# Second norm's columns and statistics taken into the scan's last stretch, one barrier fewer, scatter paced one batch later

## The chip, the cores and the metric

The program runs on one core of one Trainium2 chip. A core has five engines that run their own instruction streams and wait for each other only through semaphores: TensorE (PE, with its weight loads as PEld), VectorE (DVE), ScalarE (ACT), GpSimd (POOL) and SyncE (SP, which here only issues DMAs). The metric is the device time of one execution in microseconds (us). The kernel before takes 1730.65 us, the median of three runs (1730.52 to 1741.02).

## The reference

Four layers work on 4096 tokens (16 sequences of 256) of 128 numbers. Each layer normalises x and adds the outputs of a mixer and of a mixture of experts to it:

```
xn = _layernorm(x, axis=-1)
x = x + _L0_attn_ref(xn, ...) + _L0_ffn_ref(xn, ...)      # selective scan; 16 experts, 12 of them MLPs
xn = _layernorm(x, axis=-1)                               # the "second norm" of the title
x = x + _L1_attn_ref(xn, ...) + _L1_ffn_ref(xn, ...)      # causal attention; 9 experts, top 2
...
```

The mixer of layer 0 is a scan over each sequence. For each of 256 channels it keeps 16 states:

```
def step(h, t):
    dA_t, dBu_t, C_t = t
    h = dA_t * h + dBu_t
    return (h, jnp.einsum('bdn,bn->bd', h, C_t))
```

The router of layer 1 takes `sigmoid(xn @ gate.T + bias)` and the two largest of nine scores. What matters here: the mean and the variance of each token's 128 numbers, and the nine products of each normalised token with the router's columns.

## The kernel before

x stays in SBUF as `x_tok` (`g.x`), 32 tiles of 128 tokens by 128 numbers. A program is a row of blocks. Inside a block each engine runs its own stream; at a block's end all engines meet in a barrier. A `section` holds the semaphores of a block. When it ends it clears them, and unless it was told `last=False` it sets one more barrier behind that.

**Layer 0** (`mamba`) is one block in two parts. In its first part, the front, PE makes convolution and gate of 16 batches of 256 tokens (lines 662 and 666), ACT applies the activations of a batch (lines 812 and 814, counted in `act_done`), SP stores the gates, DVE makes the step sizes `delta`, and POOL scatters the tokens' rows to the experts' places in DRAM: 64 indirect DMAs, 56 of them in the front (line 591, issued by line 1048) and 8 between the first steps of the scan. The n-th scatter waits until ACT has done `3 + n // 5` batches, at most 16:

```
pool.wait_ge(fs.act_done, min(BATCH, 3 + n // 5))
scatter_choice(nc, pool, scattered, disp, g, r, n)
```

In its second part, the scan, there are 128 steps: 8 blocks of 512 tokens times 16 states. In a step ACT makes the decays (830, 832), POOL the inputs (613, into the space of `xn_t`), DVE the scan itself and the product with C (976, 984), and PE adds the product up in two PSUM banks (683). After 16 steps DVE multiplies by the gate (`gated`, 992), PE projects the block and adds x (`project`, 695 to 699), and ACT copies the sum back into `x_tok` (`take_out`, 846). Between the steps PE and ACT run the 12 experts. For the first seven of eight groups of four tiles the rows that the experts gave are added to x in steps 105 and later (`join`, 711 and 713; ACT's `take_joined`, 882, counted in `x_taken`). The eighth group is added by the last `project`, behind the last step.

**The second norm** (`normalise`, titled `norm1`) is the next block. PE turns the raw tiles of x on their side (270), ACT copies each four into `xn_t` (326), and PE multiplies them by the router's nine columns (255), which PE and ACT have centred before (276, 319) so that no mean has to be subtracted from x. DVE takes statistics of 32 tiles (212, 215), ACT the square root (303), DVE corrects it (220 to 224) and writes the 32 normalised tiles (233). Then DVE waits for all products (`logits_done`) and runs the router's choice, a chain of some forty short steps from line 1127 on. Behind it stand the barrier and layer 1's attention block, whose first matmuls are at line 1988. SP meanwhile loads the next weights, clears the experts' places and loads 4.9 MB of expert weights (`grouped_w`).

The order on each engine is the order in which its function is written; nothing is scheduled by a planner. PSUM has eight banks: the decays of even steps lie in banks 0 and 1, those of odd steps in 2 and 3, the sums in 4 and 5, the projection in 6.

Of the kernel before, what the change touches and what calls it, by code (L numbers as in the profile page):

```python
# [9 lines left out]
ALU = mybir.AluOpType  # L10
# [114 lines left out]
def normalise(nc, g, title, src, dst, dst_t, scale_col=None, bias_col=None, pool_job=None,  # L125
              router=None, n_exp=0, disp=None, arriving=(), router_scale=None, prefetch=None, second=None, raw=False,
              table=None, beside=None, have_stats=False):
# [5 lines left out]
    with section(nc, title, "cols_in", "stats_done", "aggr_done", "var_ready", "std_ready", "rstd_step", "xn_ready",  # L133
                 "turned", "t_ready", "job_done", "router_in", "router_scaled", "zeroed", "logits_done", "row_in", "r2_step",
                 "r2_sqrt", "xr_ready", "centre_set", "centred", "w_ready", *ROUTE, *MIX) as s:
        W = s.sb("router", [P, max(n_exp, 1)])
        wc = s.sb("router_scale", [P, 1])
        centre = s.sb("centre", [P, P]) if raw else None
# [15 lines left out]
        groups = 2 * NT // G if beside else NT // G  # L154
# [4 lines left out]
        with nc.Block() as block:  # L159

            @block.sync
            def _(sp):
# [5 lines left out]
                if router is not None:  # L168
                    sp.dma_start(W[:], router).then_inc(s.router_in, 16)
# [35 lines left out]
            def _(dve):  # L205
                if raw:
                    nc.vector.tensor_scalar(centre[:], g.ident[:], -1.0 / D, None, ALU.add).then_inc(s.centre_set, 1)
                if not have_stats:
                    for i in range(NT):
                        if arriving and i % (NT // len(arriving)) == 0:  # L210
                            dve.wait_ge(arriving[i * len(arriving) // NT], 16)
                        nc.vector.bn_stats(stats[:, i, :], src[:, i, :]).then_inc(s.stats_done, 1)
                    for i in range(NT):
                        dve.wait_ge(s.stats_done, i + 1)
                        nc.vector.bn_aggr(mv[:, i, :], stats[:, i, :]).then_inc(s.aggr_done, 1)
                    dve.wait_ge(s.aggr_done, NT)
# [33 lines left out]
            def _(pe):  # L250

                def logits(b):
                    pe.wait_ge(s.t_ready, b + 1)
# [10 lines left out]
                for i in range(NT):  # L264
                    b = i // G
                    if i % G == 0 and b >= LB:
                        pe.wait_ge(s.t_ready, b - LB + 1)
# [3 lines left out]
                    if i % G == G - 1:  # L271
# [7 lines left out]
                        if router is not None and b >= 2:  # L279
                            logits(b - 2)  # L280
                if router is not None:
                    logits(NT // G - 2)
                    logits(NT // G - 1)
                    pe.wait_ge(s.logits_done, NT // G)
                if job:
                    job.products(pe)
                    for i in range(NT):
                        if i % G == 0:
                            pe.wait_ge(s.t_ready, NT // G + max(0, i // G - LB + 2))
# [9 lines left out]
            def _(act):  # L299
# [16 lines left out]
                for b in range(NT // G):  # L316
# [3 lines left out]
                    act.wait_ge(s.turned, b + 1)  # L320
# [6 lines left out]
                    if raw and b == RAW_ROOTS:  # L327
                        roots()
                if job:
                    job.scalar(act)  # L330
                    for b in range(NT // G):
                        act.wait_ge(s.turned, NT // G + b + 1)
# [32 lines left out]
def mamba(nc, g, t, u, gate_d, delta, bc_d, r, disp, ybuf, scattered, f):  # L365
# [29 lines left out]
    JOINED = NB - 1  # L395
    with section(nc, "front", *ROUTE, "xz_ready", "gate_ready", "gate_out0", "gate_out1", "act_done", "biased", "added",
# [21 lines left out]
        with section(nc, "scan", *names, "skip_made", "zeroed", "du_ready", "bu_made",  # L418
                     "da_ready", "scan_done", "hc_ready", "sum_done", "yg_ready", "o_ready", "o_taken",
                     "gate_in", "b_in0", "b_in1", "b_in2", "b_in3", "c_in0", "c_in1", "c_in2", "c_in3", "ew_in0", "ew_in1", "ex_in0", "ex_in1", "ex_in2", "ex_in3", "turned", "xt_ready", "h_ready", "h_kept",  # L420
                     "act_done", "y_ready", "y_out", "stored0", "stored1", "weighted", "joined", "x_taken") as s:
            a_neg, d_col, w_out = f.a_neg, f.d_col, f.w_out
            d_diag = s.sb("d_diag", [P, DC, P])
# [50 lines left out]
            with nc.Block() as block:  # L474

                @block.sync
                def _(sp):
# [72 lines left out]
                    for q in range(NQ):  # L550
# [16 lines left out]
                        if q == Q_LOAD:  # L567
                            for p in range(2):
# [10 lines left out]
                def _(pool):  # L579
# [5 lines left out]
                    for n in range(2 * SCATTERED_IN_FRONT):  # L585
# [4 lines left out]
                        pool.wait_ge(fs.act_done, min(BATCH, 3 + n // 5))  # L590
# [35 lines left out]
                def _(pe):  # L626
# [144 lines left out]
                    for c in range(DC):  # L771
                        sum_states(NQ - 1, c)
                    for k in range(PIECES):
                        project(NB - 1, k)

                @block.scalar
                def _(act):
# [110 lines left out]
                    for q in range(NQ):  # L888
# [15 lines left out]
                        if j is not None:  # L904
                            take_joined(j)
                    take_out(NB - 1)

                @block.vector
                def _(dve):
# [27 lines left out]

                    job.vector(dve)
# [68 lines left out]
                    for q in range(NQ):  # L1007
# [423 lines left out]
def layer1(nc, g, t, m_out):  # L1431


    with ExitStack() as c:
# [18 lines left out]
        def prologue(loads, fill):  # L1453
            with section(nc, "mixes", "mix_in0", "mix_in1") as mixes:
# [6 lines left out]
                def pool_job(pool, rows_done):  # L1461
# [4 lines left out]
                          pool_job=pool_job, raw=True, table=ACT.Sigmoid,  # L1466
# [1468 lines left out]
def program(nc, t, out):  # L2935
    with ExitStack() as ctx:
# [16 lines left out]
        g.blank = sb("blank_rows", [P, BLANKS, ROW])  # L2953
        g.mv = sb("norm_mv", [P, NT, 2])
# [114 lines left out]
```

## Time and profile before

| | us |
|---|---|
| median of the three runs | 1730.65 |
| the profiled execution | 1731.69 |
| its span in the trace | 1729.9 |
| layer 0's front | 40.1 to 165.5 |
| layer 0's scan, 128 steps | 165.5 to 651.2 |
| from the last step to the second norm's block | 651.2 to 662.1 |
| the second norm until the router's choice begins | 662.1 to 683.4 |
| the router's choice, until layer 1's block | 683.4 to 704.1 |

The profiled execution spends 1.8 us outside the span. Times in the rows are counted from the start of the span; a row of a timeline merges instructions of one form that follow each other on an engine. "banks" is PSUM. What stands behind "idle before" names what ended the engine's wait.

### The profile page before, as it was taken

The page shows a single profiled execution, that of the slowest core. Times are in us where ns is not written, and L with a number is a line of the kernel's source. Part 1 is how long each engine was busy: PE and PEld are TensorE (multiplying, and loading weights), DVE is VectorE, ACT ScalarE, POOL GpSimd, SP SyncE. Part 2 cuts the span into 40 slices and gives each one's busy share as a digit, 9 for nine tenths or more (in the row PEclk, how much of TensorE's full clock was granted, in tenths as well). Part 3 has the DMA queues.
Part 4 walks back from the last instruction along what each step waited for, and adds up shares of the span by engine and source line. Part 5 has one row for each costly group of instructions (what it writes and reads, how often), then busy time and mean ns, then how long its engine had stood idle before and what let it go on. Part 6 is the DMA issues. An engine that isn't in the chain of part 4 may idle for free. (4 is left out here: it accounts for less than half of the span.)

```text
span 1729.9 us, 31949 instructions
## 1 busy us (share of the span) xinstructions
PE 1483.8 (86%) x11604; PEld 949.2 (55%) x11604; DVE 1228.4 (71%) x2007; ACT 957.3 (55%) x1608; POOL 766.5 (44%) x691
## 2 busy tenths in 40 slices
PE   5978698888887788678999999977999999878997
PEld 5745254444443337245799976632444444556885
DVE  7566999999999896666544468758823998565335
ACT  1147487786774672334665556644644777443441
POOL 1357787887887652476244443122400000055341
PEclk9989899999999897889999999986999999779999
DMA  4524776887877875675422246207621341311323
GB/s 148 159 56 124 183 184 176 185 195 187 177 178 157 202 154 194 178 183 91 76 63 63 56 91 96 35 24 187 101 60 37 58 70 27 140 38 49 88 77 103
DMA packets 193562, 200.93 MB, mean 116 GB/s; under 512 B 22474, under 2 KB 142569, under 8 KB 193152
## 3 DMA queue, kind: packets, MB, share of 16 engines
q1 hardware_dynamic: 181816, 177.33, 44.3%
q0 software_dynamic: 11520, 21.52, 4.6%
q8 instruction: 95, 1.56, 0.4%
q14 instruction: 59, 0.48, 0.1%
q10 hardware_dynamic: 72, 0.03, 0.0%
HBM read 144.45 MB, written 57.48 MB: 117 GB/s over the span
## 5 line engine op out<-in xcount | busy, mean ns | idle before, releaser
L613 POOL TENSOR_TENSOR xn_t<-scan_b_rows,scan_du 128x1024 f32<-128x1024 f32 x128 | 301.0, 2359 | 103.5 <-DMA scan_b_rows<-states 65.9
L683 PE MATMUL banks<-ring,ident 128*128 128x512 f32 x512 | 263.2, 628 | 69.3 <-DVE ring L984 68.5
L976 DVE TENSOR_TENSOR_SCAN banks<-banks,xn_t 128x1024 f32<-128x1024 f32 x128 | 293.0, 2289 | 17.8 <-ACT banks L832 16.2
L2455 ACT ACTIVATE att_pr<-banks 128x768 f32<-128x768 f32 (+1 forms) x256 | 234.1, 916 | 128.5 <-PE banks L2342 77.0
L683 PEld LDWEIGHTS banks<-ring,ident 128*128 128x128 f32 x512 | 90.0, 195 | 200.2 <-DVE ring L984 132.6
L832 ACT ACTIVATE banks<-delta,scan_exp_centre,a_neg 128x510 f32<-128x510 f32 x256 | 189.2, 770 | 0.3
L2503 DVE TENSOR_REDUCE att_mb<-banks 128x4 f32<-128x1024 f32 x128 | 154.0, 1221 | 17.1 <-PE banks L2309 11.9
L2358 PE MATMUL banks<-att_pr,att_vx 128*32 128x256 f32 (+1 forms) x2048 | 153.6, 371 | 8.3 <-ACT att_ot L2460 4.7
L2499 DVE TENSOR_REDUCE att_mb<-banks 128x6 f32<-128x768 f32 x128 | 121.4, 954 | 54.2 <-PE banks L2316 39.4
L984 DVE TENSOR_TENSOR ring<-banks,scan_c_rows 128x1024 f32<-128x1024 f32 x128 | 156.4, 1222 | 3.8
L1603 POOL IOTA xn_tok<- 128x32 int32 x1 | 0.2, 187 | 287.2 <-POOLq L80 287.2
L2309 PE MATMUL banks<-att_ks,att_qs 48*128 48x256 bf16 (+1 forms) x1024 | 108.7, 271 | 17.9 <-DMA att_ks<-k_parts 6.6
L1419 POOL DMA_INDIRECT ybuf<-att_yo,att_xin x72 | 69.9, 970 | 104.5 <-DVE att_yo L1403 94.9
L2334 PE MATMUL banks<-att_qs,att_ks 50*128 50x256 bf16 (+1 forms) x1024 | 107.1, 266 | 6.0 <-DMA att_qs<-att_mt 2.6
L1329 PE MATMUL banks<-att_xt,att_wc 128*128 128x128 f32 x864 | 109.8, 277 | 1.3 <-DVE att_xt L1384 1.3
L1329 PEld LDWEIGHTS banks<-att_xt,att_wc 128*128 128x128 f32 x864 | 103.5, 194 | 1.9 <-DVE att_xt L1384 1.7
L1048 POOL DMA_INDIRECT disp<-xn_tok,places x64 | 69.5, 1085 | 53.4 <-ACT u L814 34.3
L830 ACT COPY banks<-zeros 128x4 f32<-128x4 f32 x128 | 20.8, 162 | 114.3 <-DVE ring L984 114.3
L2276 POOL DMA_INDIRECT disp<-xn_tok,places x64 | 62.9, 983 | 42.3 <-issue 14.6
L2334 PEld LDWEIGHTS banks<-att_qs,att_ks 50*128 50x128 bf16 x1024 | 39.6, 94 | 60.1 <-issue 39.7
L1620 POOL DMA_INDIRECT ybuf<-gau_eyo,gau_exin x40 | 39.6, 991 | 72.6 <-DVE gau_eyo L1914 65.0
L1384 DVE COPY att_xt<-banks 128x128 f32<-128x128 f32 x72 | 20.9, 291 | 71.3 <-issue 45.7
(398 smaller groups left out, 3129.5 us busy)
## 6 DMA issues: line engine op xcount, KB each, us to landing
scan_b_rows<-states SPq DMA_DIRECT2D x128, 256.0 KB
scan_c_rows<-states SPq DMA_DIRECT2D x128, 256.0 KB
scan_ew<-f_packed SPq DMA_DIRECT2D x12, 578.0 KB
q_parts<-att_p_parts SPq DMA_DIRECT2D x16, 384.0 KB, 4.6
k_parts<-att_p_parts SPq DMA_DIRECT2D x16, 384.0 KB, 5.2
att_qs<-q_parts SPq DMA_DIRECT2D x64, 96.0 KB
att_ks<-k_parts SPq DMA_DIRECT2D x64, 96.0 KB
disp<-blank_rows SPq DMA_DIRECT2D x1, 4680.0 KB, 15.2
```

The costliest lines, as they stand in the source:

```text
L613: nc.gpsimd.tensor_tensor(bu[:, q % AHEAD], b_rows[:, q % HELD, None, :].to_broadcast([P, DC, TT]), du[:, b % 2], ALU.mult).then_inc(s.bu_ ...
L683: nc.tensor.matmul(g.ps[:, Y0 + c, :], g.ident[:], hc[:, q % RING, c], start=False, stop=(q % DS == DS - 1)).then_inc(s.sum_done, 1)
L832: ins = nc.scalar.activation(inner(decays(q)[:, c]), inner(delta[:, c, span(b)]), ACT.Exp, scale=a_neg[:, c, n:n + 1], bias=exp_centre[:])
L976: v.tensor_tensor_scan(states, states, rows(bu[:, q % AHEAD]), 0.0, ALU.mult, ALU.add).then_inc(s.scan_done, 1)
L984: v.tensor_tensor(hc[:, q % RING], decays(q), c_rows[:, q % HELD, None, :].to_broadcast([P, DC, TT]), ALU.mult).then_inc(s.hc_ready, 1)
L1329: ins = nc.tensor.matmul(g.ps[:, 4 * p + 1 + m, c * P:(c + 1) * P], wc[:, p, m, c * P:(c + 1) * P], xt[:, p, :], start=True, stop=True)
L2309: ins = nc.tensor.matmul(g.ps[:, 2 * m_slot(i) + half, lo:hi], qs[rows_of, p, j, q * P:(q + 1) * P], ks[rows_of, p, j, 0:hi - lo], start=T ...
L2334: ins = nc.tensor.matmul(g.ps[:, 2 * s_slot(i) + half, k * T:k * T + T - q0], ks[rows_of, p, j, k * P:(k + 1) * P], qs[rows_of, p, j, q0:T ...
L2358: ins = nc.tensor.matmul(g.ps[r * 32:(r + 1) * 32, O_BANK, q0:T], vx[:, b % 2, k, 4 * jg + r, :], pr[:, i % RING, half, k * T:k * T + T - q0],
L2455: nc.scalar.activation(pr[:, i % RING], g.ps[:, at:at + 2, 0:W], ACT.Exp, scale=scale).then_inc(s.p_ready, 1)
L2499: v.tensor_reduce(mb[:, b % 2, j, :].rearrange("p (g n) -> p g n", g=2), g.ps[:, at:at + 2, 0:W].rearrange("p g (n k) -> p g n k", k=P), A ...
L2503: v.tensor_reduce(mb[:, b % 2, j, :], g.ps[:, at:at + 2, :].rearrange("p g (n k) -> p (g n) k", k=T), AX_X, ALU.max).then_inc(s.m_taken, 1)
```

## The change

1. **The scan's last stretch.** A buffer `centre` and the router's columns (`next_router`, loaded by SP in step 102) are there before the scan ends. Behind the last `sum_states` PE centres the columns (line 782 of the changed kernel) and turns 28 tiles of x, that is the seven groups that have been joined by then (790): three groups ahead of the last `project`, four behind it. ACT copies them into `xn_t` (935), three groups ahead of its last `take_out` and four behind. DVE takes the statistics of those 28 tiles (1058, 1068), ten ahead of the last `gated`, the others behind it.
2. **The second norm** only turns, copies and measures the last four tiles. The products of the first 28 wait for nothing any more.
3. **One barrier.** The section of the scan ends with `last=False`.
4. **The scatter's pace.** The n-th scatter waits for `4 + n // 5` batches in place of `3 + n // 5`. No instruction moves by this; only the value that POOL waits for does.

On PE, before, from the end of the last `project` over the block's end (the two branches) into the second norm:

```order
L695 MATMUL banks<-w_out_m,front_dtx 128x128 x2
L696 MATMUL banks<-x_tok,ident 128x128
L699 MATMUL banks<-xn_tok,ident 128x128 x2
L474 UNCONDITIONAL_BRANCH
L249 UNCONDITIONAL_BRANCH [waits barrier_Pool_Activation_PE_DVE_SP_release]
L270 MATMUL banks<-ident,x_tok 128x128 x8
L276 MATMUL banks<-norm_router,norm_centre 128x9 [waits norm1_centre_set,norm1_router_in]
L270 MATMUL banks<-ident,x_tok 128x128 [waits norm1_w_ready]
L270 MATMUL banks<-ident,x_tok 128x128 x3
L255 MATMUL banks<-norm_router,xn_t 128x9 [waits norm1_t_ready]
L255 MATMUL banks<-norm_router,xn_t 128x9 x3
```

On PE, of the change, from the last `sum_states` (690) to the first of the last `project` (702):

```order
L690 MATMUL banks<-ring,ident 128x512 [waits scan_hc_ready]
L690 MATMUL banks<-ring,ident 128x512
L782 MATMUL banks<-next_router,scan_centre 128x9 [waits scan_next_in,scan_centre_set]
L790 MATMUL banks<-ident,x_tok 128x128 [waits scan_x_taken]
L790 MATMUL banks<-ident,x_tok 128x128 x3
L790 MATMUL banks<-ident,x_tok 128x128 [waits scan_x_taken]
L790 MATMUL banks<-ident,x_tok 128x128 x3
L790 MATMUL banks<-ident,x_tok 128x128 [waits scan_x_taken]
L790 MATMUL banks<-ident,x_tok 128x128 x3
L702 MATMUL banks<-w_out_m,front_dtx 128x128 [waits scan_weighted,scan_o_taken,scan_yg_ready]
```

On PE, of the change, from the last group turned over the block's end into the second norm:

```order
L790 MATMUL banks<-ident,x_tok 128x128 [waits scan_xt_kept,scan_x_taken]
L790 MATMUL banks<-ident,x_tok 128x128 x3
L480 UNCONDITIONAL_BRANCH
L251 UNCONDITIONAL_BRANCH [waits barrier_Pool_Activation_PE_DVE_SP_release]
L273 MATMUL banks<-ident,x_tok 128x128 x4
L258 MATMUL banks<-next_router,xn_t 128x9 x28
L258 MATMUL banks<-next_router,xn_t 128x9 [waits norm1_t_ready]
L258 MATMUL banks<-next_router,xn_t 128x9 x3
```

So 28 transposes have gone ahead of the barrier, 12 of them ahead of the last projection, and behind the barrier the products stand in one run.

On DVE, of the change, from the last step's product (1022) over the block's end into the second norm:

```order
L1022 TENSOR_TENSOR ring<-banks,scan_c_rows 128x1024 [waits scan_sum_done,scan_c_in3,scan_scan_done]
L1058 BN_STATS norm_stats<-x_tok 128x6 [waits scan_x_taken]
L1058 BN_STATS norm_stats<-x_tok 128x6 x9
L1030 TENSOR_TENSOR front_dtx<-banks,front_gate 128x1024 [waits scan_o_ready,scan_gate_in,scan_sum_done]
L1058 BN_STATS norm_stats<-x_tok 128x6 x18
L1068 BN_AGGR norm_mv<-norm_stats 128x2 [waits scan_stats_done] x28
L480 UNCONDITIONAL_BRANCH
L206 UNCONDITIONAL_BRANCH [waits barrier_Pool_Activation_PE_DVE_SP_release]
L214 BN_STATS norm_stats<-x_tok 128x6 x4
```

Before, the gate's product stood right behind the last step's, and all 32 BN_STATS behind the barrier.

The diff, cut to its core:

```diff
@@ normalise
+        have = ahead.groups if ahead else 0
+        left = NT // G - have
+        W = ahead.router if ahead else s.sb("router", [P, max(n_exp, 1)])
...
-                    for i in range(NT):
+                    for i in range(have * G, NT):
...
                 def logits(b):
-                    pe.wait_ge(s.t_ready, b + 1)
+                    if b >= have:
+                        pe.wait_ge(s.t_ready, b - have + 1)
...
                 if router is not None:
-                    logits(NT // G - 2)
-                    logits(NT // G - 1)
+                    for b in range(0 if have else NT // G - 2, NT // G):
+                        logits(b)
...
-                    if raw and b == RAW_ROOTS:
+                    if raw and b == max(have, RAW_ROOTS):
                         roots()
@@ mamba
+    TURN_BANKS, CENTRE_BANK = 3, 3
+    FIRST_STATS = 10
...
                         if q == Q_LOAD:
+                            sp.dma_start(g.ahead.router[:], t["f1_gate"]).then_inc(s.next_in, 16)
...
-                        pool.wait_ge(fs.act_done, min(BATCH, 3 + n // 5))
+                        pool.wait_ge(fs.act_done, min(BATCH, 4 + n // 5))
...
                     for c in range(DC):
                         sum_states(NQ - 1, c)
+                    pe.wait_ge(s.centre_set, 1)
+                    pe.wait_ge(s.next_in, 16)
+                    nc.tensor.matmul(g.ps[:, CENTRE_BANK, 0:E1], centre[:], g.ahead.router[:], start=True,
+                                     stop=True).then_inc(s.centred, 1)
+
+                    def turn(j):
+                        pe.wait_ge(s.x_taken, j + 1)
+                        if j >= TURN_BANKS:
+                            pe.wait_ge(s.xt_kept, j - TURN_BANKS + 1)
+                        for i in range(GRP):
+                            ins = nc.tensor.transpose(g.ps[:, j % TURN_BANKS, i * P:(i + 1) * P], g.x[:, j * GRP + i, :], g.ident[:])
+                        ins.then_inc(s.x_turned, 1)
+
+                    for j in range(TURN_BANKS):
+                        turn(j)
                     for k in range(PIECES):
                         project(NB - 1, k)
+                    for j in range(TURN_BANKS, JOINED):
+                        turn(j)
...
+                    def keep(j):
+                        if j == 0:
+                            act.wait_ge(s.scan_done, NQ)
+                        act.wait_ge(s.x_turned, j + 1)
+                        nc.scalar.copy(g.xn_t[:, j * GRP * P:(j + 1) * GRP * P], g.ps[:, j % TURN_BANKS, :]).then_inc(s.xt_kept, 1)
+
+                    act.wait_ge(s.centred, 1)
+                    nc.scalar.copy(g.ahead.router[:], g.ps[:, CENTRE_BANK, 0:E1]).then_inc(s.router_made, 1)
+                    for j in range(TURN_BANKS):
+                        keep(j)
                     take_out(NB - 1)
+                    for j in range(TURN_BANKS, JOINED):
+                        keep(j)
...
+                    nc.vector.tensor_scalar(centre[:], g.ident[:], -1.0 / D, None, ALU.add).then_inc(s.centre_set, 1)
                     job.vector(dve)
...
+                    dve.wait_ge(s.x_taken, JOINED)
+                    for i in range(FIRST_STATS):
+                        statistics(i)
                     gated(NB - 1)
+                    for i in range(FIRST_STATS, JOINED * GRP):
+                        statistics(i)
+                    for i in range(JOINED * GRP):
+                        dve.wait_ge(s.stats_done, i + 1)
+                        v.bn_aggr(g.mv[:, i, :], g.stats[:, i, :]).then_inc(s.aggr_done, 1)
@@ layer1, program
+        g.ahead.groups = NT // 4 - 1
+        g.ahead.router = sb("next_router", [P, E1])
```

## Rows read from the trace of the kernel before

**Rows 1.** Windows: stretch, length; PE, PEld, DVE, ACT, POOL busy (count); PEclk, DMA share, GB/s

```profile
165.50:651.20 485.70, 399.98 (x1278) 192.36 (x1278) 458.02 (x277) 339.02 (x597) 364.55 (x193) 0.97 0.77 179
651.20:662.10 10.90, 6.72 (x44) 5.24 (x45) 1.23 (x1) 0.61 (x2) 0.01 (x1) 1.00 0.00 0
662.10:683.40 21.30, 20.19 (x99) 19.38 (x99) 18.12 (x103) 7.24 (x12) 3.00 (x5) 0.56 0.67 223
695.00:701.00 6.00, 0.00 (x0) 0.00 (x0) 5.48 (x17) 0.00 (x0) 0.06 (x1) 0.53 0.61 258
```

**Rows 2.** Timeline of DVE: start, length, line, operation, count, idle before and its end

```profile
653.23 1.23 DVE L992 TENSOR_TENSOR front_dtx<-banks,front_gate 128x1024 f32<-128x1024 f32 x1 [2.08 <-PE banks L683]
662.26 6.28 DVE L212 BATCH_NORM_STATS2 norm_stats<-x_tok 128x6 f32<-128x128 f32 x32
668.45 2.20 DVE L215 BATCH_NORM_AGGREGATE norm_mv<-norm_stats 128x2 f32<-128x6 f32 x32
672.45 8.29 DVE L233 TENSOR_SCALAR xn_tok<-x_tok,norm_mv,norm_rstd 128x128 f32<-128x128 f32 x32
683.41 0.30 DVE L1127 MEMSET norm_cont<- 128x288 f32 x1 [2.67 <-PE banks L255]
```

**Rows 3.** Timeline of PE in the same stretch

```profile
651.21 1.98 PE L683 MATMUL banks<-ring,ident 128*128 128x512 f32 x4 [1.48 <-DVE ring L984]
654.51 0.71 PE L695 MATMUL banks<-w_out_m,front_dtx 128*128 128x128 f32 x4 [1.32 <-DVE front_dtx L992]
662.11 1.07 PE L270 MATMUL banks<-ident,x_tok 128*128 128x128 f32 x8 [2.87 <-PEq L80]
678.15 5.13 PE L255 MATMUL banks<-norm_router,xn_t 128*128 128x9 f32 x24
```

**Rows 4.** Timeline of ACT in the same stretch

```profile
645.42 0.59 ACT L882 COPY x_tok<-banks 128x512 f32<-128x512 f32 x1 [1.84 <-PE banks L713]
659.28 0.58 ACT L846 COPY x_tok<-banks 128x512 f32<-128x512 f32 x1 [11.80 <-PE banks L699]
662.08 1.28 ACT L311 ACT_TABLE_LOAD   x1 [2.21 <-PEq L80]
670.90 0.23 ACT L303 ACTIVATE norm_std<-norm_rstd 128x32 f32<-128x32 f32 x1 [4.60 <-DVE norm_rstd L218]
```

**Rows 5.** Waits of SP's queue from 655 to 664: us in total, times, longest

```profile
SPq L80 <- PEq L80: 1.7, 3, 0.7
```

**Rows 6.** Window of PE alone: length, busy us and count, PEclk, DMA share, GB/s

```profile
664.60:683.30 18.70, 18.64 (x88) 0.50 0.74 249
```

**Rows 7.** Timeline of POOL where the front meets the scan

```profile
153.06 0.97 POOL L1048 DMA_INDIRECT disp<-xn_tok,places  x1 [0.97 <-issue]
154.04 2.38 POOL L613 TENSOR_TENSOR xn_t<-scan_b_rows,scan_du 128x1024 f32<-128x1024 f32 x1
156.59 1.81 POOL L1048 DMA_INDIRECT disp<-xn_tok,places  x1 [0.17 <-issue]
```

**Rows 8.** Timelines of ACT and of DVE there: two batches' activations, the first step

```profile
151.45 0.83 ACT L814 ACTIVATE u<-banks,b_conv 128x256 f32<-128x256 f32 x2
160.24 0.83 ACT L814 ACTIVATE u<-banks,b_conv 128x256 f32<-128x256 f32 x2
165.53 2.30 DVE L976 TENSOR_TENSOR_SCAN banks<-banks,xn_t 128x1024 f32<-128x1024 f32 x1 [2.44 <-ACT banks L832]
```

**Rows 9.** Waits from 60 to 130: who for whom, us in total, times, longest

```profile
DVE delta L921 <- remote: 16.4, 1, 16.4
ACT front_gate L812 <- remote: 15.5, 2, 11.5
PE banks L645 <- DVE front_dtx L915: 12.2, 1, 12.2
```
**Rows 10.** Windows of POOL's scatters (L1048): length, busy us, count, PEclk, DMA share, GB/s

```profile
64.40:96.60 32.20, 24.79 (x25) 0.87 0.21 66
117.20:152.10 34.90, 26.08 (x23) 1.00 0.37 97
```

More of the change, by code:

```diff
@@ L126, in normalise @@
               router=None, n_exp=0, disp=None, arriving=(), router_scale=None, prefetch=None, second=None, raw=False,
-              table=None, beside=None, have_stats=False):
+              table=None, beside=None, have_stats=False, ahead=None):
     G = 4
@@ L135, in normalise @@
                  "r2_sqrt", "xr_ready", "centre_set", "centred", "w_ready", *ROUTE, *MIX) as s:
-        W = s.sb("router", [P, max(n_exp, 1)])
+        have = ahead.groups if ahead else 0
+        left = NT // G - have
+        W = ahead.router if ahead else s.sb("router", [P, max(n_exp, 1)])
         wc = s.sb("router_scale", [P, 1])
-        centre = s.sb("centre", [P, P]) if raw else None
+        centre = s.sb("centre", [P, P]) if raw and not have else None
         stats = g.stats
@@ L153, in normalise @@
         job = beside(s, s.sb) if beside else None
-        groups = 2 * NT // G if beside else NT // G
+        groups = NT // G + left if beside else left
         def row_bank(b):
@@ L167, in _ @@
                         n_cols += 16
-                if router is not None:
+                if router is not None and not have:
                     sp.dma_start(W[:], router).then_inc(s.router_in, 16)
@@ L205, in _ @@
             def _(dve):
-                if raw:
+                if raw and not have:
                     nc.vector.tensor_scalar(centre[:], g.ident[:], -1.0 / D, None, ALU.add).then_inc(s.centre_set, 1)
                 if not have_stats:
-                    for i in range(NT):
+                    for i in range(have * G, NT):
                         if arriving and i % (NT // len(arriving)) == 0:
@@ L263, in _ @@
                 turned_rows = src if raw else dst
-                for i in range(NT):
+                for i in range(have * G, NT):
                     b = i // G
-                    if i % G == 0 and b >= LB:
+                    if i % G == 0 and b >= LB and not have:
                         pe.wait_ge(s.t_ready, b - LB + 1)
@@ L278, in _ @@
                             pe.wait_ge(s.w_ready, 1)
-                        if router is not None and b >= 2:
+                        if router is not None and b >= have + 2:
                             logits(b - 2)
                 if router is not None:
-                    logits(NT // G - 2)
-                    logits(NT // G - 1)
+                    for b in range(0 if have else NT // G - 2, NT // G):
+                        logits(b)
                     pe.wait_ge(s.logits_done, NT // G)
@@ L315, in _ @@
                     act.wait_ge(s.cols_in, n_cols)
-                for b in range(NT // G):
+                for b in range(have, NT // G):
                     if raw and b == 2:
```

20 lines of the change are left out of this document (12 added, 8 removed).

## Prediction

> **What bounds the kernel now.** I read the windows by stage first. In the scan VectorE (DVE) is busy 458.0 of 485.7 us, TensorE (PE) 400.0 and GpSimd (POOL) 364.6 [rows 1]; the scan is bound by DVE, and the change adds nothing to its steps. Behind the last step that ends: from 651.2 to 662.1 DVE works 1.2 us of 10.9, and in the second norm until the routing begins PE is busy 20.2 of 21.3 us [rows 1]. These two stretches, 32 us in all, are what the change works on, and a timeline shows what ends last in each.
>
> The first stretch is a chain: the last step's product releases the sums, which run from 651.21 to 653.19, DVE's `gated` 653.23 to 654.46, the projection from 654.51, ScalarE's (ACT) last copy 659.28 to 659.86 [rows 2 to 4]. Until 662.1 nothing computes: that is three barriers, seen in SP's waits as three of 1.7 us together, longest 0.7 [rows 5]. In the second stretch DVE is done with its normalised rows at 680.74 (672.45 + 8.29) and then waits 2.67 us for the router's products, whose last 24 passes end at 683.28; the routing starts at 683.41, 21.3 us behind the block's start [rows 2, 3]. So PE bounds this stretch, with DVE 2.7 us behind it.
>
> **The change, part by part.** The sum is made against the profiled execution, 1731.69 us, which lies 1.04 above the median.
>
> *End of the scan.* PE gets one matmul of nine columns and 12 turns between the last sums and the last projection. Eight turns at the full clock took 1.07 us [rows 3], so 12 take 1.6. They start at 653.2 where PE idled for 1.32 us [rows 3], and end at about 654.8 in place of 654.51: +0.3 on the chain. What they wait for is there: the seventh group was added to x by 646.0 [rows 4]. The projection then ends 0.3 later, at 659.55, and ACT's own last copy at 660.13. Behind it stand four more copies of 512 columns. A copy of that size takes 0.58 [rows 4], PE's sixteen turns (2.1 us) run ahead of them, so ACT ends at 660.13 + 4 x 0.58 = 662.45 in place of 659.86: **+2.6**. Were the projection's turns late behind each copy (three banks, four groups) it would be a few tenths more; if PE's turns fit wholly in the gap, 2.3.
>
> DVE's additions cost nothing here. Statistics took 6.28 / 32 = 0.196 each [rows 2]; ten are 1.96 us and lie in the 2.08 us in which DVE waited for the last sums [rows 2]. Eighteen more (3.5) and 28 aggregations of 2.20 / 32 = 0.069 (1.9) run from 654.5 to about 660, under the projection and 2.4 us ahead of ACT's end. Were that cover gone they would cost 5.4. The three early copies on ACT (1.74) and the router's copy lie in its 11.80 us of idleness ahead of 659.28 [rows 4]. The centre is one DVE instruction at the front's start, in a pause. The router's columns are one more small DMA on SP's queue in step 102, far from any use.
>
> *One barrier fewer.* Three waits of 1.7 us are 0.57 each, the longest 0.7: **-0.6** (bounds -0.5 and -0.7) [rows 5]. The next block starts at 662.45 + 1.6 = 664.1, two microseconds later than before.
>
> *The second norm.* DVE's path: four statistics and aggregations 1.1 us. The root follows later: ACT loads a table (1.28) and now copies the last group (0.58) ahead of the roots, so the root starts at about 2.1 and takes 0.23; DVE's rows began 1.32 behind the root's end (671.13 to 672.45) and last 8.29 [rows 2, 4]. That gives 2.1 + 0.23 + 1.32 + 8.29 = 11.9 behind the block's start: the earliest the routing can begin.
>
> PE's path: four turns (0.55), then 64 passes of nine columns (two per tile) without a wait but one. Their price hangs on the clock. Before, the granted clock was 0.50 from 664.6 on (1.2 GHz of the two levels, 1.2 and 2.4), although PE was busy 18.64 of 18.70 us [rows 6]; the mean of 0.56 over the whole 21.3 us [rows 1] leaves 1.00 for the first 2.5. At 0.50 a pass took 5.13 / 24 = 0.214 us [rows 3]; at full clock I estimate half, 0.107. All at full clock: 0.55 + 6.85 + 0.13 (from the last product to the routing's first instruction, as before) = 7.5, and DVE's 11.9 is what counts. All at half: 1.0 + 13.7 + 0.13 = 14.8. With the clock falling 2.5 us after the block's start as before: 18 passes by then, 46 x 0.214 = 9.85 after, 2.5 + 9.85 + 0.13 = 12.5. I take this, since the same kind of work stands behind the same pause of PE: 12.5 in place of 21.3, **-8.8** (bounds -9.4 and -6.5).
>
> The Trainium skill ("TensorE: Matmul & The Clock Gate", section "Part 1: The HAM clock gate (the "warmup" mystery)") has the clock full while TensorE is busy and halved when it idles. By that the products, now back to back, would run at full clock and DVE would end last, at 11.9. The trace does not agree: 0.50 at 18.64 busy of 18.70 us [rows 6]. The two differ by 0.6 us in the sum.
>
> *The scatter's pace.* POOL issues the last front scatter at 153.06 and then its first scan product, behind which wait ACT's decays and DVE [rows 7]. With the new number this scatter waits for batch 14, whose activations end at 161.07 in place of batch 13's 152.28; POOL started 0.78 behind that signal [rows 7, 8]. So 161.85 + 0.97 + 2.38 = 165.2 for the first product, and DVE's first scan is at 165.53 [rows 7, 8]: 0.3 of slack. If that scatter takes the 1.81 of the one at 156.59 [rows 7] the slack is gone and 0.5 is lost; the next products follow with their scatters between them, and up to 1.5 may be lost until POOL has its lead. I take **+0.1** (0 to +1.5): before, a scatter that no DVE operation slowed took 0.97. Behind the waiting scatter on POOL stand only the later scatters, one IOTA and the scan's inputs. The experts read the scattered rows after scatter 63, between the scan's steps as before, with no gap that the scan waits on.
>
> *The sum.* +2.6 - 0.6 - 8.8 + 0.1 = -6.7; bounds from -7.9 (+2.3, -0.7, -9.4, 0, rounded) to -2.8 (+2.7, -0.5, -6.5, +1.5). 1731.69 - 6.7 = 1725.0 for an execution like the profiled one, and 1724.0 against the median of 1730.65.
>
> **The rivals.**
>
> *The clock stays full in the products* (the skill's reading). DVE ends the stretch at 11.9: -9.4 in place of -8.8, 1723.4 us. For it: nothing interrupts the products now. Against it: the half clock at 99.7% busy [rows 6].
>
> *The front gets shorter.* In the front there is one place where signals come late: ACT's gates wait "remote" for 15.5 us (11.5 at once), DVE's `delta` 16.4, and in the end PE stands still for 12.2 us [rows 9]. In the same stretch POOL issues 25 scatters without a pause, 24.8 us of 32.2 [rows 10]. With the new number POOL stops after about 15 of them until batch 6 is through. If the run of scatters makes the signals late, the pause takes it away: up to -12.2, 1724.0 - 12.2 = 1711.8; half of it 1718. For it: the two coincide. Against it: a later run of 23, as dense (26.1 of 34.9 us) [rows 10], shows no such wait, and nothing in the rows names the cause.
>
> *Slower: the late signals come again at the front's end.* The scatters now reach until 162.8, beside batches 13 to 15, which before had POOL's scan products beside them. If the signals of one of those batches come late as here, by up to 12.2 us, the scan starts that much later: 1736.2. It decides for slower once the lateness is over 6.7 us. Against it: the 23 scatters between 117 and 152 [rows 10] have none beside them.
>
> *The gain is given back behind the norm.* The routing's chain is unchanged (683.4 to 704.1), so layer 1's attention starts 6.8 us earlier, but the 4.9 MB of expert weights move at 258 GB/s, a DMA share of 0.61, until about 701 [rows 1]. Those DMAs are issued by SP from the norm's start on, which is 2 us later, so up to 6 us of them run beside the attention's first loads, and what these wait is lost: between 1728 and 1731. For it: the attention's block began 3 us behind the last of these transfers. Against it: its first matmuls use what is in SBUF.
>
> That the change does nothing is hardly a rival: the wait it takes away ends last in its stretch.
>
> **How the numbers follow.** The forecast 0.45 (its own range 1722 to 1728), the full clock 0.17, a shorter front 0.18, gain handed back 0.10, late signals at the front's end 0.10. From 1711.8 to 1731 the cases but the last hold 0.90; the range 1710 to 1733 leaves out the last and the far end of the shorter front. About 1% (17 us) is what a measurement of this kernel can tell from no change; a gain of over 17.3 (below 1713.3) needs the whole of the front's 12.2, so faster has 0.10, slower than 1748 has 0.02, and no change of that size 0.88.
>
> **What would show it.** In the changed kernel's trace: the centring matmul and 12 turns between the last sums and the projection, and the projection's start at most 0.5 us later against the sums; ACT's last copy of turned columns 2.4 us behind its `take_out`, as the last work of the block; 1.6 us to the next block; the routing's first memset 12.5 us behind that block's start with the granted clock at 0.50 in most of the products (11.9 and 1.00 by the first rival); POOL's last front scatter at about 161.9 and the first scan step at 165.5. Wrong would be: products waiting on copies, "remote" waits of the gates at another place, or an attention that begins with waits on DMA.

## The result, and the profile after

The changed kernel takes 1719.03 us, the median of six runs (1717.39 to 1721.75), against 1732.73 for six runs of the kernel before (1730.52 to 1741.02). The ratio is 0.9924 with a 95% interval of 0.9896 to 0.9952: faster by three quarters of a per cent, inside what the forecast called no change. 1724.0 was forecast, with 1710 to 1733 as its range.

The profiled execution took 1717.39 us, its span is 1715.6, 14.3 below that of the kernel before. By stage, with the boundaries of the table ahead of the prediction:

| stage | before | after | difference | forecast |
|---|---|---|---|---|
| first norm | 40.1 | 37.2 | -2.9 | 0 |
| front of layer 0 | 125.4 | 118.2 | -7.2 | +0.1 |
| scan | 485.7 | 485.1 | -0.6 | 0 |
| last step to the second norm's block | 10.9 | 12.7 | +1.8 | +2.0 |
| second norm until the routing | 21.3 | 14.4 | -6.9 | -8.8 |
| routing, until layer 1's block | 20.7 | 20.6 | -0.1 | 0 |
| all behind it | 1025.8 | 1027.4 | +1.6 | 0 |

So the two stretches that the forecast was about gave 5.1 us where 6.8 were forecast, and the front, forecast at nothing, gave the most.

DVE's timeline of the changed kernel, as in [rows 2] (start, length, line, operation, count, idle before and its end):

```profile
640.43 2.02 DVE L1058 BATCH_NORM_STATS2 norm_stats<-x_tok 128x6 f32<-128x128 f32 x10
642.59 1.22 DVE L1030 TENSOR_TENSOR front_dtx<-banks,front_gate 128x1024 f32<-128x1024 f32 x1
643.73 3.57 DVE L1058 BATCH_NORM_STATS2 norm_stats<-x_tok 128x6 f32<-128x128 f32 x18
647.22 1.94 DVE L1068 BATCH_NORM_AGGREGATE norm_mv<-norm_stats 128x2 f32<-128x6 f32 x28
656.52 8.29 DVE L235 TENSOR_SCALAR xn_tok<-x_tok,norm_mv,norm_rstd 128x128 f32<-128x128 f32 x32
667.63 0.30 DVE L1177 MEMSET norm_cont<- 128x288 f32 x1 [2.82 <-PE banks L258]
```

PE's, as in [rows 3]:

```profile
640.57 1.98 PE L690 MATMUL banks<-ring,ident 128*128 128x512 f32 x4 [1.48 <-DVE ring L1022]
642.53 1.51 PE L790 MATMUL banks<-ident,x_tok 128*128 128x128 f32 x12
643.87 0.71 PE L702 MATMUL banks<-w_out_m,front_dtx 128*128 128x128 f32 x4
648.43 2.05 PE L790 MATMUL banks<-ident,x_tok 128*128 128x128 f32 x16
653.23 0.81 PE L273 MATMUL banks<-ident,x_tok 128*128 128x128 f32 x4 [2.75 <-PEq L80]
653.84 13.66 PE L258 MATMUL banks<-next_router,xn_t 128*128 128x9 f32 x64
```

And ACT's, as in [rows 4]:

```profile
648.63 0.59 ACT L870 COPY x_tok<-banks 128x512 f32<-128x512 f32 x1 [3.82 <-PE banks L706]
649.12 2.06 ACT L935 COPY xn_t<-banks 128x512 f32<-128x512 f32 x4
653.20 1.28 ACT L314 ACT_TABLE_LOAD   x1 [2.02 <-PEq L80]
```

The statistics lie where they were put, in the wait for the sums and under the projection, and DVE is done at 649.16, two microseconds ahead of ACT. ACT ends the stretch with its four copies. In the norm DVE still waits for the products, 2.82 us, so PE still ends that stretch: 64 passes in 13.66 us are 0.213 each, the price at half clock from the first to the last. The windows of PE alone, as in [rows 6], show it:

```profile
653.20:653.55 0.35, 0.32 (x3) 0.99 0.00 0
653.55:667.60 14.05, 13.99 (x68) 0.50 0.53 171
```

In the front, the waits of the changed kernel between 60 and 130 us stand against [rows 9]: there PE stood still for 12.2 us behind late signals, and DVE waited 16.4 in `delta`. PE's long wait is gone and DVE's is 8.5 us (with no releaser that the profile can name), but ACT's gates still wait. A wait ends "remote" when the profile finds no instruction that ended close to the signal. In the kernel before, the matmuls that the 16.4 us wait was for had ended at 81.40 (79.52 + 1.88), 12.2 us before DVE went on:

```profile
79.52 1.88 PE L645 MATMUL banks<-front_dtx,front_w_dt 128*128 128x512 f32 x4
93.59 1.41 DVE L921 TENSOR_SCALAR delta<-banks,front_b_dt 128x512 f32<-128x512 f32 x2 [16.37 <-remote]
```

The changed kernel's waits:

```profile
ACT front_gate L836 <- remote: 18.9, 3, 8.3
DVE delta L958 <- issue: 9.9, 2, 8.5
DVE front_dtx L952 <- remote: 3.5, 1, 3.5
```

The first norm is the same code in both kernels. Its last 24 passes, first before and then after:

```profile
33.80 5.14 PE L255 MATMUL banks<-norm_router,xn_t 128*128 128x16 f32 x24
```

```profile
28.21 2.75 PE L258 MATMUL banks<-norm_router,xn_t 128*128 128x16 f32 x24
```

In the changed kernel's trace the clock rose at 22.1 us, in the middle of this norm, and in that of before not until 43.4. Fourteen traces were taken in all. Twelve of them (the changed kernel's second one too) have a first norm of 39.9 to 40.3 us up to the barrier's end, two have 37.1 and 37.3. So these 2.9 us are chance, and not the change.

### The profile page after: what moved, and what is told of

The parts are those of the page before. It is cut to its first block and busy times, and to the rows that moved or that the text cites. A ratio compares the mean times of both kernels' runs of the same rounds, so it can differ in the third digit from the quotient of the medians.

```text
span 1715.6 us, 31943 instructions
## 1 busy us (share of the span) xinstructions
PE 1472.1 (86%) x11604; PEld 938.8 (55%) x11604; DVE 1223.3 (71%) x2007; ACT 957.4 (56%) x1608; POOL 771.3 (45%) x691
## 5 line engine op out<-in xcount | busy, mean ns | idle before, releaser
L620 POOL TENSOR_TENSOR xn_t<-scan_b_rows,scan_du 128x1024 f32<-128x1024 f32 x128 | 306.9, 2404 | 89.9 <-DMA scan_b_rows<-states 60.9
L2553 DVE TENSOR_REDUCE att_mb<-banks 128x4 f32<-128x1024 f32 x128 | 153.9, 1221 | 20.7 <-PE banks L2359 15.5
L2359 PE MATMUL banks<-att_ks,att_qs 48*128 48x256 bf16 (+1 forms) x1024 | 108.7, 270 | 20.1 <-DMA att_ks<-k_parts 10.9
```

The lines of the kernel that those rows point to most:

```text
L620: nc.gpsimd.tensor_tensor(bu[:, q % AHEAD], b_rows[:, q % HELD, None, :].to_broadcast([P, DC, TT]), du[:, b % 2], ALU.mult).then_inc(s.bu_ ...
L2359: ins = nc.tensor.matmul(g.ps[:, 2 * m_slot(i) + half, lo:hi], qs[rows_of, p, j, q * P:(q + 1) * P], ks[rows_of, p, j, 0:hi - lo], start=T ...
L2553: v.tensor_reduce(mb[:, b % 2, j, :], g.ps[:, at:at + 2, :].rearrange("p g (n k) -> p (g n) k", k=T), AX_X, ALU.max).then_inc(s.m_taken, 1)
```

## The experiments

**The front: the pace, or chance.** Two kernels tell it apart: the kernel before with the new pace alone, and the changed kernel with the old one.

```diff
-                        pool.wait_ge(fs.act_done, min(BATCH, 3 + n // 5))
+                        pool.wait_ge(fs.act_done, min(BATCH, 4 + n // 5))
```

> The kernel before with the scatter's new pace alone (4 + n // 5). Theory A: the pace shortens layer 0's front, by the 7 us by which it was shorter in the changed kernel's trace (118.3 against 125.4 us from the first norm's end to the scan's first step); the time is then 7 us below the kernel before (ratio about 0.996), and the front in this trace is about 118 us. Theory B: the front's length varies from one execution to the next, and the pace does nothing; the ratio is 1.000 within 0.001, and the front may be anything from 118 to 126 us. In both, the second norm is as in the kernel before: 21.3 us until the routing.

The ratio to the kernel before is 0.9960 (0.9935 to 0.9985; twelve runs, median 1727.35 against 1733.65), the front 116.8 us, the second norm 21.4 as before.

The same line turned round in the changed kernel:

> The changed kernel with the old pace (3 + n // 5) put back. Theory A (the pace shortens the front): about 7 us slower than the changed kernel, 1726 us against 1719, front about 125 us. Theory B (chance): as the changed kernel, about 1719 to 1721 us. The stretch from the last step to the second norm's block stays 12.7 us and the norm until the routing 14.4 us, as in the changed kernel's trace, unless the clock of TensorE stays full in the products (then 11.9).

Ratio 0.9966 (0.9941 to 0.9992; median 1730.11), front 122.1. The two ratios multiplied give 0.9926, the changed kernel's own. Either half of the change is worth a good third of a per cent, and the pace is a cause by itself: theory A, with the size to be read from more traces (below).

**What in the scatters costs.** The changed kernel with the front's scatters left out, and the changed kernel once more:

```diff
...
-                    for n in range(2 * SCATTERED_IN_FRONT):
+                    for n in (NT,):
...
-                        pool.wait_ge(fs.act_done, min(BATCH, 4 + n // 5))
-                        scatter_choice(nc, pool, scattered, disp, g, r, n)
```

> The changed kernel without the 56 scatters of the front (it leaves out their rows, so the experts work on blank rows; 8 scatters between the scan's first steps stay). Theory A (late signals of TensorE in the front come from the scatters that GpSimd issues beside): no wait for a late signal is left in the front, and the front is shorter than the changed kernel's 118.3 us, by 5 to 12 us. Theory B (the late signals have another cause): 'remote' waits of the gates stay, about 15 us in all, and the front stays at 118 us or a little under.

> The changed kernel once more, for a second trace. If the front's 118.3 us belong to the kernel, it is within 1 us of them here; if they are chance, anything from 117 to 126 us. The first norm until the front took 37.1 us in the changed kernel's trace and 40.0 in that of before, with the same code: if that is chance (the clock of TensorE rose in the middle of it in one and behind it in the other), either of the two comes up. The second norm until the routing: 14.4 us if the clock falls at the block's start again, 12 to 13 if it falls later.

Without scatters the front takes 108.9 us (39.9 to the first step's 148.77) and no wait of it ends "remote". The largest waits from 41 to 150 us and the first step of the scan:

```profile
POOL xn_t L617 <- PE banks L639: 65.8, 1, 65.8
ACT front_gate L833 <- PE banks L670: 37.6, 11, 5.3
POOL xn_tok L1087 <- DVEq L1263: 23.2, 1, 23.2
DVE delta L955 <- PE banks L649: 19.5, 5, 4.9
ACT front_gate L833 <- DMA gate<-front_gate: 9.2, 1, 9.2
```

```profile
148.77 2.30 DVE L1011 TENSOR_TENSOR_SCAN banks<-banks,xn_t 128x1024 f32<-128x1024 f32 x1 [4.37 <-ACT banks L853]
```

The second trace of the changed kernel has a front of 117.9 and again late signals (22.6 us in four waits of ACT's gates). So the late signals of PE come from the scatters that POOL issues beside: theory A. Whether POOL's issuing or the transfers themselves delay them is not told apart, since this kernel has neither. All fronts together, from the end of the barrier to the first scan:

| pace | fronts, us | mean |
|---|---|---|
| 3 + n // 5 | 125.5, 122.1, 120.5 | 122.7 |
| 4 + n // 5 | 118.3, 118.2, 117.9, 116.9, 116.8, 116.8, 116.5 | 117.3 |
| no scatter in the front | 108.9 | |

The pace is worth 5.4 us by the means; the profiled pair showed 7.2. What it takes away is DVE's part of the late signals. From the barrier to the first scan step, DVE's waits that end "remote" or without a releaser add up to 28.7 to 30.4 us in the three traces with the old pace and to 9.4 to 20.4 in the seven with the new one. PE's longest wait at the matmuls of the step sizes is 12.2, 4.2 and 7.4 us with the old pace and at most 3.0 with the new one. ACT's gates show no such order (19.3 to 28.1 against 9.5 to 32.1 us).

**Later still.** If a later start helps, more of it should help more; if pauses between the scatters do it, six to a batch should not.

```diff
-                        pool.wait_ge(fs.act_done, min(BATCH, 4 + n // 5))
+                        pool.wait_ge(fs.act_done, 5 + n // 6)
```

> The changed kernel with the pace 5 + n // 6 in place of 4 + n // 5: the scatters begin one batch later and then go six to a batch. Traces so far: front 125.5 and 122.1 us with 3 + n // 5, 116.8 to 118.3 with 4 + n // 5, 108.9 without scatters. Theory A (it is the late start of the run that helps, since the scatters then meet fewer of TensorE's signals): front 113 to 116 us and the kernel 2 to 4 us below the changed one. Theory B (it is the pauses between scatters that let the signals through; six to a batch of 8 us at 1.28 us each leave hardly one): front 117 to 122 us, no gain or a loss.

> The changed kernel with the pace 6 + n // 6: begins two batches later, six to a batch, and its last two scatters wait for batch 14, as one does in the changed kernel. Theory A (the late start): front 111 to 115 us. Theory B (the pauses): 117 to 122 us. In both, if GpSimd is last at the scan's start, one scatter more stands ahead of its first product: 1.3 us.

(The second has 6 + n // 6.) Fronts of 117.7 and 116.8, ratios 0.9945 (0.9909 to 0.9980) and 0.9978 (0.9951 to 1.0005): the first as theory B had it, the second between the two, and no gain over the changed kernel in either. With 6 + n // 6 the trace shows why a front with fewer late signals need not end earlier. ACT's gates waited 0.7 us "remote" where they waited 22.1 in the changed kernel (DVE's `delta` still 10.7 in two waits), and ACT was through its 16 batches at 108.1 us of the front. But POOL, which had begun its scatters 8.3 to 8.8 us later than in the changed kernel's three traces, ended them last. ACT's last batch, POOL's last front scatter and first product, and DVE's first step in this trace:

```profile
147.30 0.83 ACT L838 ACTIVATE u<-banks,b_conv 128x256 f32<-128x256 f32 x2
153.41 0.97 POOL L1098 DMA_INDIRECT disp<-xn_tok,places  x1 [0.30 <-issue]
154.38 2.37 POOL L620 TENSOR_TENSOR xn_t<-scan_b_rows,scan_du 128x1024 f32<-128x1024 f32 x1
156.86 2.30 DVE L1014 TENSOR_TENSOR_SCAN banks<-banks,xn_t 128x1024 f32<-128x1024 f32 x1 [12.39 <-POOL xn_t L620]
```

All 56 scatters ran there in one row with a single stop of 2.2 us (0.30 us between most of them), so it is not for lack of pauses that ACT's early batches are late: the times went as theory B said, but its mechanism is not what the trace shows. That the start counts is likely and not shown: with 5 + n // 6, which begins 4.0 to 4.5 us later than the changed kernel, the gates again waited 15.0 us. And the profiled execution of the kernel with 6 + n // 6 took 1715.93 us, the median of its ten runs is 1728.41; what the others lost is not in a trace and stays open.

**The barrier.** The kernel before with one barrier fewer:

```diff
-                     "act_done", "y_ready", "y_out", "stored0", "stored1", "weighted", "joined", "x_taken") as s:
+                     "act_done", "y_ready", "y_out", "stored0", "stored1", "weighted", "joined", "x_taken", last=False) as s:
```

> The kernel before with the scan's section ending without its barrier, and nothing else. Theory A (three barriers of 0.57 us each, as the forecast had it): from the last step's end to the second norm's block 10.85 us becomes 10.3. Theory B (a barrier's own handshake is 0.25 us, and the rest of each is GpSimd clearing semaphores, which stays): 10.6.

The stretch took 10.60, theory B. ACT's last copy ends at 651.05 and its next instruction starts at 653.02, 1.97 us later, where the kernel before had 2.22 (659.86 to 662.08) [rows 4]:

```profile
650.47 0.58 ACT L846 COPY x_tok<-banks 128x512 f32<-128x512 f32 x1 [11.80 <-PE banks L699]
653.02 1.28 ACT L311 ACT_TABLE_LOAD   x1 [1.96 <-PEq L80]
```

SP's waits in that stretch, this kernel:

```profile
SPq L80 <- PEq L80: 1.5, 2, 1.2
```

Two waits in place of three [rows 5], but the longest is now 1.2 us, not 0.7: in it POOL clears the semaphores of both sections, which it had done in two waits. A barrier less saves its handshake, 0.25 us. This kernel ran once, but the stretch repeats closely: 10.85 us in the two traces that have the old norm and all three waits, 12.61 to 12.63 in the eight with all 64 passes in the new norm.

**The clock in the products.** The forecast let the clock fall 2.5 us after the block's start; it fell at 0.35. One kernel takes the first group's products (8 of 64 passes) ahead of the block's end; another puts all turns ahead of the projection, so that PE ends on the projection as before.

```diff
...
                     for j in range(TURN_BANKS, JOINED):
                         turn(j)
+                    pe.wait_ge(s.router_made, 1)
+                    for j in range(g.ahead.done):
+                        pe.wait_ge(s.xt_kept, j + 1)
+                        for i in range(j * GRP, (j + 1) * GRP):
+                            nc.tensor.matmul(g.ps[:, EB, i * E1:(i + 1) * E1], g.xn_t[:, i * P:(i + 1) * P], g.ahead.router[:],
+                                             start=True, stop=True)
...
```

> The changed kernel with the router's products of the first group (8 of 64 passes) made behind the last turns, ahead of the block's end. At the full clock they take 0.9 us there and TensorE ends at most 0.3 us behind ScalarE: the stretch from the last step to the block 12.6 to 12.9 us. In the second norm 8 passes fewer at 0.213 us: 13.8 to 14.5 becomes 12.1 to 12.8 us until the routing if the clock is half in all products as before. If the products ahead keep the clock full for longer, down to 11.7, where VectorE ends last.

Stretch 12.70, norm 12.05 until the routing, with the clock falling 1.23 us after the barrier. In the timed run below 12.71 and 11.74, with the fall at 1.58. A third trace with these products ahead, the one with another pace below, has the fall at 0.27 and a norm of 12.93, so they do not keep the clock up. PE in the timed run:

```profile
650.29 0.63 PE L273 MATMUL banks<-ident,x_tok 128*128 128x128 f32 x4 [2.05 <-PEq L80]
650.75 11.03 PE L258 MATMUL banks<-next_router,xn_t 128*128 128x9 f32 x56
```

The turns first:

```diff
-                    for j in range(TURN_BANKS):
+                    for j in range(JOINED):
                         turn(j)
                     for k in range(PIECES):
                         project(NB - 1, k)
-                    for j in range(TURN_BANKS, JOINED):
-                        turn(j)
...
```

> The changed kernel with all 28 turns and their copies ahead of the last projection, so that TensorE runs the projection last before the block's end, as in the kernel before. The stretch from the last step to the second norm's block grows from 12.6 to about 13.2 us (ScalarE's seven copies stand between). In the kernel before, alone or with the pace or without the barrier, the clock fell 2.56 to 2.74 us after the block's start, in the changed kernel 0.42 to 1.23. Theory A (what TensorE ran ahead of the barriers sets when the clock falls): it falls 2 us or more after the start, and the norm takes about 13 us until the routing. Theory B (the back-to-back products of nine columns set it): it falls 0.4 to 1.3 us after the start, as in the changed kernel, and the norm takes 13.7 to 14.5 us.

The clock fell 1.11 us after the barrier, the norm took 13.86 us, and PE's products read like the changed kernel's:

```profile
653.67 0.63 PE L273 MATMUL banks<-ident,x_tok 128*128 128x128 f32 x4 [2.68 <-PEq L80]
654.13 13.16 PE L258 MATMUL banks<-next_router,xn_t 128*128 128x9 f32 x64
```

So theory A falls: it is not the projection that kept the clock up. (The stretch itself took 12.60, not 13.2: with ACT's copies all ahead of the projection nothing stands behind `take_out`.) Over the eight traces with all 64 passes in the norm the fall came 0.42 to 1.21 us after the barrier, and the norm took from 14.50 (fall at 0.42) down to 13.78 us (at 1.21), 0.9 us less for each microsecond of full clock. Carried on to 2.5 us this gives 12.6, the 12.5 of the forecast. In the three kernels with the old norm the fall came at 2.55 to 2.73.

Theory B's figures came, but its cause does not hold either: the clock can fall before the first of these products. In the changed kernel it fell at 653.55 and the first product began at 653.84. In the kernel before it fell 2.5 us into the block, and the first product came 0.9 us later:

```profile
662.10:664.60 2.50, 1.49 (x11) 1.00 0.13 22
665.48 1.72 PE L255 MATMUL banks<-norm_router,xn_t 128*128 128x9 f32 x8
```

Both falls follow a pause of PE at the block's end (2.75 and 2.87 us). Why nearly the same pause is followed by an earlier fall in the new norm stays open. What the traces do show is that the products, once the clock has fallen, run at half clock to their end.

**A better version.** The first group's products ahead, timed; the same with 6 + n // 6 and 54 front scatters; and the changed kernel beside them.

> The changed kernel with the first group's products ahead of the block's end, as looked at before (stretches of 12.70 and 12.05 us in place of 12.6 and 13.8 to 14.5), now timed: 1.7 us below the changed kernel, too little to be told from it by the times; the ratio to the kernel before 0.990 to 0.994.

> The first group's products ahead, the pace 6 + n // 6, and 54 in place of 56 scatters in the front (10 in place of 8 between the scan's first steps). With 6 + n // 6 no signal of TensorE was late before the last batches (ScalarE was through batch 15 at 108.1 us of the front, 114 to 115 in the changed kernel), but GpSimd ended its 56 scatters last. Two scatters fewer give 2.6 us: front 114 to 115 us against 116.5 to 118.3. If the experts' first tokens then come late for step 10, up to 3 us are lost in the scan (481 to 485 us). Together with the products ahead 4 us below the changed kernel; if the pace helps nothing, 1.7.

> The changed kernel, timed on the same chip beside the two variants. Ratio to the kernel before 0.990 to 0.995, front 116.5 to 118.5 us, stretch to the second norm 12.6 us, the norm until the routing 13.8 to 14.5 us.

| kernel | median | ratio to the kernel before | front | to the block | norm |
|---|---|---|---|---|---|
| first group ahead | 1713.95 | 0.9912 (0.9878 to 0.9946) | 116.9 | 12.71 | 11.74 |
| and 6 + n // 6, 54 scatters | 1721.06 | 0.9943 (0.9920 to 0.9965) | 117.9 | 12.70 | 12.93 |
| the changed kernel | 1720.06 | 0.9931 (0.9904 to 0.9958) | 118.2 | 12.62 | 14.16 |

With the group ahead the two stretches take 24.8, 24.5 and 25.6 us in the three traces, against 26.4 to 27.1 in the changed kernel's three. Part of that is the time of the clock's fall: on the line of norm against fall from the eight traces above, each of the three norms lies 1.7 us lower, 8 passes at 0.213, as expected. The intervals of the times overlap and can't show it. The other pace gives nothing again: in this front POOL had its first product made early (it began at 111.7 us of the front), but a signal of PE's last batches came late, ACT ended at 115.0 us, and the scan started at 117.9.

## Why the prediction was right, and where its steps were off

**Right in the whole, partly for reasons that it had put elsewhere.** The range held the time and the forecast lay 5 us above it. The sum itself did not hold: the two stretches that it was about gave 5.1 us of 6.8, and the front, put at +0.1, gave 5 to 7. That the range held is owed to the rival of the shorter front, which had set its lower end, and that the forecast came so near is in part luck. Term by term:

*The scatter's pace*, "I take +0.1", is the step that failed. What it looked at held: the last front scatter issued at 151.95 us, 114.9 behind the barrier, waiting for batch 14, and POOL's first product ended at 155.29, ACT's first decays at 155.28, so the wait at the end cost nothing (forecast was 0.3 us of slack, and both ended together). What it had left to a rival with 0.18 was the early burst. The rival "the front gets shorter" was the right mechanism in part: late signals come from the scatters, and of its 12.2 us the pace gave 5.4 on average. Its own counter-evidence, the later run of scatters beside which nothing was late [rows 10], did not carry; the kernel without scatters shows that such evidence from one trace was too little.

*The late signals at the front's end* were the rival on the slower side. They do occur. In the changed kernel's trace ACT's batch 14 waited 3.22 us for a signal:

```profile
149.85 0.60 ACT L836 ACTIVATE front_gate<-banks 128x512 f32<-128x512 f32 x1 [3.22 <-remote]
```

That is a part of the gain given back, far from the 6.7 us from which it would have decided.

*The second norm*, -8.8, was mis-sized by the clock: -6.9 in the profiled pair, -6.9 to -7.6 over eight traces. The formula held (a pass 0.213 us at half and 0.112 at full clock against 0.214 and 0.107, DVE's rows ended at 664.81, 11.6 behind the block's start against 11.9 worked out); the time of the fall did not. "The same kind of work stands behind the same pause" was the weak sentence: the work behind the pause had changed, and the fall came at another time, though no run shows that the one is the cause of the other.

*The clock stays full* fell: 0.50 in 13.99 busy of 14.05 us. So the rule of the Trainium skill ("TensorE: Matmul & The Clock Gate", "Part 1: The HAM clock gate (the "warmup" mystery)"), full while busy, does not describe these nine-column products. In the first norm of the changed kernel the 24 passes of sixteen columns did run at full clock, once it had risen.

*The end of the scan*: +2.6 for ACT's copies was 1.96 (8.71 to 10.67 us from the last step's end to ACT's end). The 0.3 for PE's turns did not come, the projection starts 3.36 us behind the last step in both, because `gated` still ends last ahead of it (643.81 in the changed kernel); and copies that follow each other come every 0.49 us ((651.18 - 649.22) / 4), not 0.58, since a timeline's length of one copy overlaps the next. The barrier was 0.2, not 0.6: dividing SP's three waits by three counted POOL's clearing of semaphores as barrier. Together +1.8 against +2.0, right by two errors that cancel.

*The gain handed back behind the norm*: up to the end of the barrier the routing took 20.3 to 20.5 and the stages behind it 1025.6 to 1036.5 us in all traces, of either kernel, with no order in it; no sign of this rival, and no proof against a microsecond or two.

## What to carry to other kernels

A stretch between two blocks is worth filling with work whose inputs are there, but ask which engine then ends it, and price a following run of narrow products at half clock unless a trace of that very order shows otherwise. Where one engine issues many indirect DMAs beside a pipeline of others, look for waits that end "remote", and leave the DMAs out once to see what they cost: here 8.4 us of the front (117.3 against 108.9). A barrier's price is the time that vanishes when it is taken out, not its share of a wait.

## What the runs showed of the hardware

While GpSimd issued indirect DMAs, signals of TensorE reached ScalarE and VectorE late: waits that ended "remote" took up to 18.5 us (ACT's gate in the changed kernel with the old pace), and by the trace the matmuls waited for had ended up to 16.0 us before (DVE's `front_dtx` in the kernel before, 83.24 to 99.20). No wait ended so when the DMAs were left out (front 108.9 against 117.3 us). Which batches are hit, and why a run as dense beside other batches hits none, stays open. TensorE's clock rose in the first norm in two of fourteen traces at 22.1 and 22.4 us and else only behind it, which moves 2.9 us of the kernel by chance. An all-engine barrier ahead of another one costs 0.2 to 0.25 us.
